# Sliding-window attention and mixture of experts on one core: the value product in 64x64 tiles over two units and two PSUM banks

## Chip, cores and metric

One Trainium2 chip; the kernel runs on 1 core. The metric is the device time of one execution in microseconds (us), smaller is better. Engines are named as in the profile: PE (TensorE), DVE (VectorE), ACT (ScalarE), POOL (GpSimd), SP (the queue that issues most DMAs).

## The reference

```python
# x: (2, 2048, 256) f32; 16 heads of 64; window of 128 keys; 8 experts, top 2
mod = silu(c) @ wmod                     # six rows per batch: shift, scale, gate, twice
h = layernorm(x) * (1 + ca) + sa
q, k, v = split(h @ Wqkv)
scores = q @ k.T * 64 ** -0.5            # key j counts for query i when i-127 <= j <= i
out = softmax(scores) @ v
x = x + ga * (out @ Wout)
h = layernorm(x) * (1 + cb) + sb
x = x + gb * moe(h)                      # gate, top 2 of 8, 640 slots per expert and choice, two products with relu
```

## The kernel before

The 4096 tokens are 8 chunks of 512 (4 tiles of 128). For each chunk the attention runs over 16 units. A unit is a pair of heads j over one half of the chunk: two heads by two query tiles, so four blocks of 128 queries. A block sees 256 keys: the 128 keys before its tile and the 128 of its tile. Exactly half of these 256 are inside the window: key p of the tile before where p > query, key p of the tile itself where p <= query. In the last chunk the units are ordered by half of the chunk first.

There is no scheduler. Each engine has its own instruction stream, written out by hand as a loop over steps i = 4 to 19 in the function `chunk`, and semaphores tie them together. In step i of a chunk before the last:

- **PE** (line 765): `scores` of unit i (fp32, a head's 64 dimensions on one half of the rows, 64 queries on one half of the columns: four 64x64 tiles at once), `weighted_values` of unit i-4, `transposes` of unit i-2 (four 128x128 fp32 transposes of the probabilities into the bank `pt`), then one q or k projection of the next chunk and, in steps 12, 13, 14 and 16, one v projection. Steps 12 and 15 have the router's logits and counts of the chunk before. Behind the last step come four v projections and `project_out`.
- **DVE** (line 1267): in even steps first `attn_low` of a finished pair; then `merge` (i), `invert_sum` (i-1), `row_max` (i), `normalise` (i-1); then what the step has of routing or layer norm (`norm_rows` in step 6, `route_tokens` in 8, `ln_shift` in 9 and 10, `route_softmax` and `route_top` in 13, `route_slots` in 16).
- **ACT** (line 971): `exponentials` (i-1), in odd steps `attn_high`, then `copy_probT` (i-2) from `pt` to SBUF, then the projections' copies out of PSUM. In steps 9 and 11 it also packs 1024 columns for the router and the layer norm.
- **POOL** (line 1438): `split_keys` (i-3), two masked copies of the 512 columns of `probT` into `probT_split` (keys of the tile, keys before it); `route_scale` in 6, `route_shift` in 7, `route_low` in 9, a layer norm part in 12, two scatters a step from 16 on.

The value product (lines 651 to 678) puts v (128 keys, 64 dimensions) in the array as 128x64 tiles, head 0 in the left columns and head 1 in the right, and streams the probabilities: first the middle 256 columns of `probT_split` for both query tiles at once, then the two outer blocks of 128. All 128 keys of every block are multiplied, the masked halves as zeros. It writes the one bank `pv`; a pair of units fills its 512 columns, and only then ACT takes the high half (`attn_high`, 512 columns) and DVE the low half (`attn_low`, 512 columns). The first product of the next pair waits for that:

```python
elif part == 0:
    at_least(pe, attn_lo, PAIRS * c + j)
```

The projections, the logits, the counts and the output products alternate between the two banks `gen0` and `gen1` in the order of the list `chunk_groups` (line 298). `claim` makes PE wait until the group two places back in that list has been copied out of PSUM:

```python
bank, before = group(c, name)
at_least(pe, gen_free[bank], before)
```

The last chunk (c = 7) has leftover projections in steps 4 to 14, and its first output group `("out", 0)` is opened in step 12 and read out by DVE (`add_attention`) in step 14. When its units are done the experts follow, and fill the rest of the time.

## Time and profile before

| | |
|---|---|
| runs | 1147.83, 1148.39, 1149.66 us; median 1148.39 us |
| profiled execution | 1147.24 us, of which the span of the core is 1144.4 us |
| granted TensorE clock, mean | 0.991 |
| busy: PE, DVE, ACT, POOL | 95%, 66%, 58%, 44% of the span |
| attention | about 54 to 691 us of the span: chunks 0 to 5 some 81 to 83 us each, chunk 6 74 us, the last chunk after it |
| experts | from 707 us |

Busy shares are averages over stages with different limits. A matmul's recorded duration includes its way through the array, and neighbours overlap, so the cost of a group on PE is read from the start of one group to the start of the next. In the timelines below the first column is the start in us from the beginning of the span, the second the time from the first start to the last end of the instructions on that row; in brackets the idle time ahead of it on its engine and who ended it.

### The profile page before, as it was taken

Reading aid. Unit: us, or ns where it says so; the run is one execution under the profiler, and the core shown is the slowest. Engines: PE = TensorE matmul, PEld = TensorE weight load, DVE = VectorE, ACT = ScalarE, POOL = GpSimd, SP = SyncE. Lnnn points to the kernel's source line nnn. Section 1 sums busy time; section 2 is a strip of 40 time slices with the busy share of each in tenths; the row PEclk is TensorE's granted clock in tenths of the full one; section 3 lists DMA queues with packets and bytes.
Section 4 is the critical chain, followed back from the end, with each engine's and each line's share of the span. In section 5 each row is a group of like instructions: output and inputs, shape, how many; then the busy total and the mean of one; then the engine's idle time right before and its main releaser. Section 6 shows DMA issues by size and latency. Waiting matters only on the chain.

```text
span 1144.4 us, 25293 instructions
## 1 busy us (share of the span) xinstructions
PE 1084.4 (95%) x9469; PEld 711.8 (62%) x9469; DVE 750.3 (66%) x1663; ACT 660.5 (58%) x1874; POOL 506.2 (44%) x555
## 2 busy tenths in 40 slices
PE   7999999999999999999998885989999999999996
PEld 4455655655655655655656564756776858585765
DVE  5776586586576585674675784756676766666653
ACT  5677476476476476476473853447474563727461
POOL 2234274365275365355445655434344352525342
PEclk9999999999999999999999998999999999999998
DMA  9744111112021021021031024434345353534000
GB/s 335 151 163 138 40 29 48 38 37 52 27 45 48 24 46 45 24 45 39 24 103 48 5 83 121 92 94 81 109 94 153 97 112 111 112 112 78 23 20 9
DMA packets 140114, 87.41 MB, mean 76 GB/s; under 512 B 96708, under 2 KB 130650, under 8 KB 139868
## 3 DMA queue, kind: packets, MB, share of 16 engines
q1 hardware_dynamic: 129244, 64.29, 21.4%
q0 software_dynamic: 10752, 21.54, 6.6%
q8 instruction: 75, 1.23, 0.5%
q14 instruction: 43, 0.35, 0.1%
HBM read 40.02 MB, written 33.79 MB: 64 GB/s over the span
## 4 chain that ended last, share of the span: by engine, by line
PE 75%; issue 7%; DVE 7%; ACT 6%; POOL 4%; DMA 0%; SPq 0%; POOLq 0%; DVEq 0%; ACTq 0%
PE down L1617 18%; PE up L1603 17%; PE gen L600 10%; PE gen L614 7%; PE gen L691 6%; PE score L637 4%; PE pv L668 4%; PE pt L648 4%; ACT prob L909 4%; PE pv L675 3%; DVE prob L1121 2%; POOL h L370 1%; POOL probT_split L1424 1%; PE gen L699 1%; POOL probT_split L1422 1%
## 5 line engine op out<-in xcount | busy, mean ns | idle before, releaser
L1643 ACT ACTIVATE hid<-up,b1T 128x512 f16<-128x512 f32 (+2 forms) x192 | 124.3, 648 | 182.1 <-PE up L1603 180.3
L1603 PE MATMUL up<-xT,w 128*128 128x512 f16 (+2 forms) x1152 | 212.5, 346 | 10.9 <-issue 10.9
L1617 PE MATMUL down<-w,hid 128*128 128x256 f16 x1920 | 213.7, 274 | 3.2 <-DVE hid L1659 3.2
L1422 POOL TENSOR_SCALAR_AFFINE_SELECT probT_split<-probT 128x512 f32<-128x512 f32 x128 | 102.9, 804 | 250.9 <-ACT probT L917 247.4
L1617 PEld LDWEIGHTS down<-w,hid 128*128 128x128 f16 x1920 | 188.6, 98 | 27.6 <-DVE hid L1659 3.7
L600 PE MATMUL gen<-hT,big 128*128 128x512 f16 x768 | 185.0, 380 | 0.6 <-DVE hT L1371 0.6
L909 ACT ACTIVATE prob<-score,negmax 128x128 f32<-128x128 f32 x512 | 180.7, 375 | 0.7 <-DVE negmax L1113 0.7
L1603 PEld LDWEIGHTS up<-xT,w 128*128 128x128 f16 x1152 | 112.9, 98 | 104.9 <-issue 12.8
L1702 POOL DMA_INDIRECT out<-y,tail x80 | 82.4, 1031 | 206.1 <-DVE y L1687 193.2
L1659 DVE TENSOR_TENSOR hid<-hid 128x512 f16<-128x512 f32 (+2 forms) x192 | 115.2, 606 | 72.4 <-ACT hid L1644 72.0
L917 ACT ACTIVATE probT<-pt 128x512 f32<-128x512 f32 x128 | 76.9, 601 | 99.0 <-PE pt L648 98.8
L1109 DVE COPY_PREDICATED score<-above,score 128x512 f32<-128x512 int32 x112 | 77.5, 692 | 77.3 <-PE score L637 77.2
L1644 ACT ACTIVATE hid<-up,b1T 128x512 f32<-128x512 f32 (+2 forms) x192 | 124.8, 650 | 0.0
L600 PEld LDWEIGHTS gen<-hT,big 128*128 128x128 f16 x768 | 73.8, 98 | 67.7 <-issue 1.2
L637 PE MATMUL score<-k,q 64*64 64x192 f32 (+2 forms) x2048 | 111.0, 330 | 2.6 <-issue 2.2
L909 ACT ACTIVATION_READ_ACCUMULATOR prob<-score,negmax 128x1 f32 x512 | 111.0, 217 | 0.0
L1692 POOL DMA_INDIRECT kept<-out,tail x80 | 86.5, 1081 | 47.6 <-issue 30.0
L1121 DVE TENSOR_TENSOR prob<-prob,rinv 128x512 f32<-128x512 f32 x128 | 103.4, 808 | 0.0
L668 PE MATMUL pv<-probT_split,v 128*64 128x256 f32 x512 | 83.5, 403 | 19.0 <-DVE attn L1134 7.0
L637 PEld LDWEIGHTS score<-k,q 64*64 64x64 f32 x2048 | 64.5, 132 | 53.9 <-issue 51.6
L614 PE MATMUL gen<-big,hT 128*128 128x512 f16 x384 | 89.1, 379 | 2.3 <-DVE logit L1160 1.2
L1424 POOL TENSOR_SCALAR_AFFINE_SELECT probT_split<-probT 128x512 f32<-128x512 f32 x128 | 86.3, 674 | 0.0
(159 smaller groups left out, 1442.4 us busy)
## 6 DMA issues: line engine op xcount, KB each, us to landing
big<-in_L_ffn_W SPq DMA_DIRECT2D x14, 1024.0 KB, 6.9
slot_inputs<-empty_row SPq DMA_DIRECT2D x80, 129.5 KB, 2.3
out<-x SPq DMA_DIRECT2D x7, 512.0 KB, 3.3
x<-in_L_attn_x SPq DMA_DIRECT2D x1, 3072.0 KB, 22.8
k<-k SPq DMA_DIRECT2D x48, 64.0 KB, 1.9
kept<-out,tail POOLq DMA_INDIRECT x80, 3.1
out<-y,tail POOLq DMA_INDIRECT x80, 2.4
x<-in_L_attn_x SPq DMA_DIRECT2D x2, 512.0 KB, 6.9
```

The source lines that it names most:

```text
L600: mm = pe.matmul(dst[:], wqkv[:, kd, a, col:col + P], hT[:, cn % 2, kd, b, :], start=(n == 0), stop=(n == 5))
L614: mm = pe.matmul(dst[:], hT[:, cn % 2, kd, a, s * P:(s + 1) * P], wqkv[:, kd, b, 2 * INNER + half * 512:2 * INNER + (half + 1) * 512], sta ...
L637: mm = pe.matmul(dst[lo:lo + HALF, 2 * hd + i, first:lo + P + HALF], q[r:r + DH, j, b * P + lo:b * P + lo + HALF], k[r:r + DH, j, b * P + ...
L668: mm = pe.matmul(pv[r:r + DH, 2 * part * P:(2 * part + 2) * P], v[:, 2 * part + 1, h * DH:(h + 1) * DH], probT_split[:, par, 2 * hd:2 * hd ...
L909: mm = act.activation(prob[:, h % 2, b, :], score[h % 2][:, b, P:], ACT.Exp, bias=negmax[:, h % 2, b:b + 1], accum_out=rowsum[:, h % 2, b: ...
L1121: dve.tensor_tensor(prob[:, h % 2], prob[:, h % 2], rinv[:, h % 2, :].unsqueeze(2).to_broadcast([P, TILES, P]), ALU.mult)\
L1422: pool.affine_select(out=probT_split[:, h % 2, :, 1], in_=probT[:, h % 2], pattern=[[0, TILES], [1, P]], compare_op=ALU.is_ge, fill=zero, ...
L1603: mm = pe.matmul(bank, w1[:, par, kd, a, ft * P:(ft + 1) * P], part_rows(e, n, xT[:, par, b * KD + kd, :]), start=(i == 0), stop=(i == 5))
L1617: mm = pe.matmul(down[n][:, s, :], hid[:, ft, a, t * P:(t + 1) * P], w2[:, par, ft, b, :], start=(i == 0), stop=(i == 3 * FT - 1))
L1643: act.activation(part_rows(e, n, hid[:, ft, 0, :]), bank, ACT.Relu, scale=1 / W_SCALE, bias=bias).then_inc(hid_hi, 1)
L1644: act.activation(part_bank(e, n, hid32[:, k_ % 4, :]), bank, ACT.Relu, scale=1 / W_SCALE, bias=bias).then_inc(up_out, 1)
L1659: dve.tensor_tensor(part_rows(e, n, hid[:, ft, 1, :]), part_bank(e, n, hid32[:, k_ % 4, :]), part_rows(e, n, hid[:, ft, 0, :]), ALU.subtra ...
```

## The change

It does six things.

1. The value product is cut into 64 keys by 64 dimensions. `high_keys` are keys 64 to 127, `low_keys` keys 0 to 63. Where a 64x64 quarter of a block is wholly masked it is left out: high keys of the tile itself see only queries 64 to 127, low keys of the tile before only queries 0 to 63. So a block's four products have 128, 64, 128 and 64 columns.
2. In one step PE runs the high keys of unit i-4 mixed, one by one, with the low keys of unit i-5 (`half_values`), so that all four quarters of the array have work, and the two halves of the rows write to different banks. In the first step of a chunk only the new unit is there; in the last step the mixed product comes ahead of the scores and the last unit's low keys alone behind them.
3. `pv` becomes two banks, one unit each (256 columns). ACT's and DVE's part is done for every unit (`attn_high_part`, `attn_low_part`), one step later than before, DVE's at the head of every step. A product waits for the low half of the unit two back.
4. For the second `pv` bank, `pt` goes: the transposes are groups of the `gen` banks now, ahead of the step's other groups.
5. `probT` goes: ACT copies the transposes straight into slot 1 of `probT_split`, a ring of three units, and POOL masks from there, the second time in place.
6. The v projections of steps 12, 13, 14, 16 move to 13, 14, 16, 17; `keep_v` from step 12 to 13. The last chunk keeps the old product of 128x64 tiles, with the new banks. (The key copies that the change's short name speaks of are transfers of the sync queue before and after.)

```diff
-                        if c == LAST:
-                            at_least(pe, attn_lo, PAIRS * c + u)
-                        elif part == 0:
-                            at_least(pe, attn_lo, PAIRS * c + j)
+                        at_least(pe, attn_lo, n_unit - 1)
...
+                    def high_keys(c, u, hd, i, cur):
...
+                        first = HALF * cur
+                        return pe.matmul(pv[n_unit % 2][r:r + DH, i * P + first:(i + 1) * P], v[HALF:, b + cur, h * DH:(h + 1) * DH],
+                                         probT_split[HALF:, n_unit % RING, 2 * hd + i, cur, first:], start=(i == 0 and cur == 0),
+                                         stop=False, skip_group_check=True)
...
+                    def low_keys(c, u, hd, i, cur):
...
+                        last = P if cur else HALF
+                        return pe.matmul(pv[n_unit % 2][r:r + DH, i * P:i * P + last], v[0:HALF, b + cur, h * DH:(h + 1) * DH],
+                                         probT_split[0:HALF, n_unit % RING, 2 * hd + i, cur, 0:last], start=False,
+                                         stop=(cur == 0), skip_group_check=True)
...
+                        for i in range(2):
+                            for n in range(2):
+                                for hd in range(2):
+                                    if new is not None:
+                                        high = high_keys(c, new, hd, i, n)
+                                    if old is not None:
+                                        low = low_keys(c, old, 1 - hd, i, 1 - n)
...
+                            if not last and i == STEPS[-1]:
+                                half_values(c, i - HI_AT, i - LO_AT)
                             if i < H or not last:
                                 scores(c, i)
-                            weighted_values(c, i - 4)
+                            if last:
+                                weighted_values(c, i - HI_AT)
+                            elif i < STEPS[-1]:
+                                half_values(c, i - HI_AT, i - LO_AT if i >= LO_AT else None)
+                            else:
+                                half_values(c, None, H - 1)
                             if i - 2 < H or not last:
-                                transposes(c, i - 2)
+                                transposes(H * c + i - 2, c, ("pt", i))
...
                         for i in STEPS:
-                            if i >= 6 and i % 2 == 0 and not last:
-                                attn_low(c, (i - 6) // 2)
+                            if i > LO_AT and not last:
+                                attn_low_part(c, i - LO_AT - 1)
```

**How the order moves.** Three places, as the instruction streams have them; line numbers are each kernel's own.

DVE, chunk 2, step 6 and the head of step 7, before (L237 is `norm_rows`; L1109, L1117, L1113 and L1121 are merge, invert_sum, row_max and normalise; L1134 is `attn_low`):

```order
L1134 TENSOR_TENSOR attn<-pv,attn 128x512 [waits attn_hi]
L1109 COPY_PREDICATED score<-above,score 128x4x128 [waits scores_done]
L1117 RECIPROCAL rinv<-rowsum 128x4 [waits exp_done]
L1113 TENSOR_REDUCE negmax<-score 128x4 [waits merged]
L1121 TENSOR_TENSOR prob<-prob,rinv 128x512 [waits rinv_ready]
L237 TENSOR_SCALAR h<-x,meanvar,rstd 128x256 [waits r_rstd]
L237 TENSOR_SCALAR h<-x,meanvar,rstd 128x256 x3
L1109 COPY_PREDICATED score<-above,score 128x4x128 [waits scores_done]
```

The same place after (L1291 is `attn_low_part`):

```order
L1291 TENSOR_TENSOR attn<-pv,attn 128x256 [waits attn_hi]
L1158 COPY_PREDICATED score<-above,score 128x4x128 [waits scores_done]
L1166 RECIPROCAL rinv<-rowsum 128x4 [waits exp_done]
L1162 TENSOR_REDUCE negmax<-score 128x4 [waits merged]
L1170 TENSOR_TENSOR prob<-prob,rinv 128x512 [waits rinv_ready]
L236 TENSOR_SCALAR h<-x,meanvar,rstd 128x256 [waits r_rstd]
L236 TENSOR_SCALAR h<-x,meanvar,rstd 128x256 x3
L1291 TENSOR_TENSOR attn<-pv,attn 128x256 [waits attn_hi]
L1158 COPY_PREDICATED score<-above,score 128x4x128 [waits scores_done]
```

Behind the routing work of every step there now stands a low half that PE waits for, also in the odd steps.

PE, chunk 2, step 12, before (L648 transposes, L740 logits, L600 a q projection, L614 a v projection):

```order
L648 MATMUL pt<-identf,prob 128x128 [waits probT_ready,norm_ready]
L648 MATMUL pt<-identf,prob 128x128 x3
L740 MATMUL gen<-gate,h2T 128x8 [waits gen_free0,turned]
L740 MATMUL gen<-gate,h2T 128x8 x23
L600 MATMUL gen<-hT,big 128x512 [waits gen_free1]
L600 MATMUL gen<-hT,big 128x512 x5
L614 MATMUL gen<-big,hT 128x512 [waits gen_free0]
L614 MATMUL gen<-big,hT 128x512 x5
L637 MATMUL score<-k,q 64x192 [waits exp_done]
```

The same place after, where the last rows show the mixed product behind the scores:

```order
L654 MATMUL gen<-identf,prob 128x128 [waits gen_free0,norm_ready]
L654 MATMUL gen<-identf,prob 128x128 x3
L783 MATMUL gen<-gate,h2T 128x8 [waits gen_free1,turned]
L783 MATMUL gen<-gate,h2T 128x8 x23
L607 MATMUL gen<-hT,big 128x512 [waits gen_free0]
L607 MATMUL gen<-hT,big 128x512 x5
L644 MATMUL score<-k,q 64x192 [waits exp_done]
L644 MATMUL score<-k,q 64x192 x7
L674 MATMUL pv<-probT_split,v 64x128 [waits cur_ready,attn_lo,prev_ready,high_done]
L683 MATMUL pv<-probT_split,v 64x128
L674 MATMUL pv<-probT_split,v 64x128
```

The projection waits for the bank that the same step's transposes filled a moment before. Step 15 has the same with the counts in place of the logits.

PE, last chunk, steps 13 and 14, after (L742 is the output product into `("out", 0)`, which lies in `gen0`):

```order
L742 MATMUL gen<-wout,attn 128x256 [waits attn_lo]
L742 MATMUL gen<-wout,attn 128x256 x26
L644 MATMUL score<-k,q 64x192 [waits exp_done]
L644 MATMUL score<-k,q 64x192 x7
L712 MATMUL pv<-probT_split,v 64x256 [waits attn_lo,cur_ready,prev_ready]
L712 MATMUL pv<-probT_split,v 64x256
L718 MATMUL pv<-probT_split,v 64x128 x4
L654 MATMUL gen<-identf,prob 128x128 [waits gen_free0,norm_ready]
```

The transposes of step 14, which had a bank of their own, now wait until DVE has read the output group out.

## Rows read from the trace of the kernel before

**Rows 1.** Windows: busy us of each engine (count), clock, DMA share, GB/s
```profile
140.00:220.00 80.00, 78.32 (x756) 48.28 (x758) 52.87 (x130) 49.98 (x177) 41.11 (x47) 1.00 0.13 34
```
**Rows 2.** Waits of PE in chunk 2, 218.7 to 302.05
```profile
PE pv L668 <- POOL probT_split L1424: 0.8, 2, 0.6
PE pv L668 <- DVE attn L1134: 0.7, 2, 0.5
PE gen L614 <- DVE logit L1160: 0.2, 1, 0.2
```
**Rows 3.** Timeline of PE, chunk 3, step 4 and the next step's start
```profile
302.06 0.88 PE L637 MATMUL score<-k,q 64*64 64x192 f32 x16
302.87 0.65 PE L668 MATMUL pv<-probT_split,v 128*64 128x256 f32 x4
303.35 0.61 PE L675 MATMUL pv<-probT_split,v 128*64 128x128 f32 x8
303.89 0.66 PE L648 MATMUL pt<-identf,prob 128*128 128x128 f32 x4
304.38 1.46 PE L600 MATMUL gen<-hT,big 128*128 128x512 f16 x6
305.77 0.55 PE L637 MATMUL score<-k,q 64*64 64x192 f32 x7
```
**Rows 4.** Timeline of PE, chunk 4, step 4: narrower score tiles at a batch's start
```profile
385.16 0.77 PE L637 MATMUL score<-k,q 64*64 64x64 f32 x16
385.86 0.65 PE L668 MATMUL pv<-probT_split,v 128*64 128x256 f32 x4
```
**Rows 5.** Groups by line and form: busy us, mean ns of one
```profile
L931 ACT ACTIVATE attn<-pv 128x256 f16<-128x256 f32 x16 | 6.3, 391 | 21.0 <-PE pv L675 21.0
...
L1246 DVE TENSOR_TENSOR attn<-pv,attn 128x256 f16<-128x256 f32 x16 | 6.7, 418 | 2.3 <-ACT attn L931 2.3
```
**Rows 6.** Timeline of ACT, chunk 3, step 5, whose scores start at 309.48
```profile
311.36 0.22 ACT L909 ACTIVATION_READ_ACCUMULATOR prob<-score,negmax 128x1 f32 x1
312.01 0.60 ACT L917 ACTIVATE probT<-pt 128x512 f32<-128x512 f32 x1 [0.43 <-PE pt L648]
```
**Rows 7.** Timeline of DVE, the same step
```profile
311.61 0.18 DVE L1117 RECIPROCAL rinv<-rowsum 128x4 f32<-128x4 f32 x1 [0.48 <-ACT prob L909]
...
312.29 0.68 DVE L1121 TENSOR_TENSOR prob<-prob,rinv 128x512 f32<-128x512 f32 x1
```
**Rows 8.** Timeline of PE, chunk 2: scores of step 6, values of steps 8, 9
```profile
226.15 0.88 PE L637 MATMUL score<-k,q 64*64 64x192 f32 x16
...
235.07 0.65 PE L668 MATMUL pv<-probT_split,v 128*64 128x256 f32 x4 [0.61 <-POOL probT_split L1424]
...
239.02 0.65 PE L668 MATMUL pv<-probT_split,v 128*64 128x256 f32 x4 [0.17 <-POOL probT_split L1424]
```
**Rows 9.** Timeline of DVE, chunk 2: norm_rows of step 6, normalise and ln_shift of 10
```profile
229.55 1.38 DVE L237 TENSOR_SCALAR h<-x,meanvar,rstd 128x256 f32<-128x256 f32 x4
...
244.77 1.12 DVE L1121 TENSOR_TENSOR prob<-prob,rinv 128x512 f32<-128x512 f32 x1
245.81 1.62 DVE L1080 SCALAR_TENSOR_TENSOR xn<-xn,rstd,kept 128x256 f32<-128x256 f32 x2
```
**Rows 10.** Timeline of POOL, chunk 2: route_scale, and the select after route_shift
```profile
231.02 2.37 POOL L370 TENSOR_TENSOR h<-h,modrow 128x1024 f32<-128x1024 f32 x1 [4.02 <-DVE h L237]
...
238.34 0.63 POOL L1424 TENSOR_SCALAR_AFFINE_SELECT probT_split<-probT 128x512 f32<-128x512 f32 x1
```
**Rows 11.** Timeline of DVE, chunk 2, step 13: route_top, then attn_low of step 14
```profile
259.00 0.18 DVE L1175 TENSOR_REDUCE lsum<-logit 128x4 f32<-128x32 f32 x1
...
261.16 0.69 DVE L1134 TENSOR_TENSOR attn<-pv,attn 128x512 f16<-128x512 f32 x1
```
**Rows 12.** Timeline of PE, last chunk, step 14
```profile
675.97 0.66 PE L648 MATMUL pt<-identf,prob 128*128 128x128 f32 x4
```
**Rows 13.** Timeline of DVE, last chunk, step 14: add_attention reads the output group
```profile
677.36 0.68 DVE L1142 SCALAR_TENSOR_TENSOR gated<-gen,modrow 128x512 f32<-128x512 f32 x1
```

More of the change, by code:

```diff
@@ L325, in group, with turned_in @@
                 return bank, opened[c][bank] + before
+            def turned_in(n_unit):
+                c, i = divmod(n_unit - 2, H)
+                return group(-1, ("pt", n_unit)) if n_unit < 2 else group(c, ("pt", i + LAG))
             def starts_batch(c, b):
@@ L846, in attention_tensor @@
                     pe.wait_ge(mod_row, 1)
-                    transposes(0, 0)
+                    transposes(0, -1, ("pt", 0))
                     scores(0, 2)
@@ L906, in exponentials @@
                         act.wait_ge(maxed, u + 1)
-                        at_least(act, pt_done, u - 1)
+                        if u >= 2:
+                            bank, before = turned_in(u - 2)
+                            act.wait_ge(gen_full[bank], before + 1)
                         for b in range(TILES):
@@ L976, in chunk @@
                             if last:
-                                attn_high_part(c, i - 4)
-                            if i % 2 == 1 and not last:
-                                attn_high(c, (i - 5) // 2)
+                                attn_high_part(c, i - HI_AT)
+                            if i >= LO_AT and not last:
+                                attn_high_part(c, i - LO_AT)
                             if last and i - 2 < H:
@@ L1277, in chunk @@
                                 keep_first_keys((i - LAG) // 2)
-                            if i == 12 and not last:
+                            if i == 13 and not last:
                                 keep_v(c, 0)
@@ L1309, in chunk @@
                         if not last:
-                            attn_low(c, PAIRS - 1)
+                            for u in range(H - 2, H):
+                                attn_low_part(c, u)
                             keep_v(c, 1)
```

131 lines of the change are left out of this document (72 added, 59 removed).

## Prediction

> **What bounds the kernel now.** First the windows: in a stretch of the middle chunks PE is busy 78.3 of 80 us, DVE 52.9, ACT 50.0 and POOL 41.1 [rows 1]. PE is the bound there. Then the waits of PE: in the 83 us of chunk 2 only 1.7 us are waits, for POOL's selects, DVE's low half and the logits' bank [rows 2]. So what is taken off PE arrives in full, as long as it isn't waited away again. The change touches the attention alone (chunks 0 to 6 in full, the last in its banks); the experts behind it stay as they are. Third the timeline of one step, from start to start [rows 3]: scores 0.81, value product 0.48 + 0.54 = 1.02, transposes 0.49, one projection 1.39, in all 3.71 us.
>
> **The value product.** The price of a column in fp32: at a batch's start two of the four passes of a score group are 128 columns wide in place of 192, and the group takes 0.70 in place of 0.81 us [rows 3, 4]. So 128 columns cost 0.11 us, 0.83 ns each, and a pass costs what its widest tile costs. (Every fp32 product is two passes; the records count them.) A score group is 4 passes of 192, 768 columns, 0.64 us; measured 0.81. The value product is now 2 passes of 256 and 4 of 128, 1024 columns, 0.85 us; measured 1.02. So each group that changes the tile's shape pays some 0.17 us, a first load and a drain.
> The mixed product has, for each quarter of the array, passes of 128, 128, 64, 64 and the same again: 768 columns, 0.64 us. It has the scores' shape and follows them directly, so the two pay 0.17 once: 0.64 + 0.64 + 0.17 = 1.45 for 1.83. That is 0.38 us a step, and a step of 3.33. What isn't shown is a pass of 64 columns. Its bounds: 0.05 us as its columns say, or 0.11 as a pass of 128, if the next load doesn't fit under it; then the product takes 8 x 0.107 = 0.85. I take the first, because the transposes, 128 columns loaded for 128 streamed, run four in 0.49 us [rows 3], hardly more than their 0.43 of columns: a load fits under as many columns as it loads.
> Sixteen steps in seven chunks give 112 x 0.38 = 42.6 us. The skew costs one product more in each chunk (first high, last low alone), 7 x 0.64 = 4.5. **38 us of work go from PE, if nothing else becomes late.**
> The rule that speaks against this is in the Trainium skill, TensorE: Matmul & The Clock Gate, Part 3, "Packing small matmuls": a weight load overlaps a running matmul only where it goes to another row group. In the mixed product all quarters are busy, so by that rule each of the eight passes would show its load.
>
> **What ACT, DVE and POOL get.** DVE's low half goes from one of 512 columns per pair, 0.69 [rows 11], to two of 256 at 0.42 [rows 5], under 0.1 us more per step; ACT's high half likewise, at 0.39. Both engines have that much room under PE's 3.33 [rows 1]. POOL's two selects stay.
> But their order now matters. In a quiet step ACT's exponentials end 2.1 us after the scores' start (309.48), DVE inverts at 2.13, normalises from 2.81 to 3.49 [rows 6, 7], and the low half of 0.42 ends at 3.9. The product of the next step is due at 3.33 + 0.70 = 4.03. There is 0.1 us to spare, where before a low half was due only every second step. So **all that DVE does in a step behind the normalisation is now waited for in full, in odd steps too**. Once PE has waited, DVE is ahead by as much in the next step.
>
> **A middle chunk, wait by wait** (chunk 2; times from the scores of step 6, 226.15 [rows 8]):
> - Step 7: `norm_rows` starts at 3.40 and takes 1.38 [rows 9], then the low half, done at 5.15; the product is due at 4.03. Wait 1.1.
> - Steps 8 and 9: `norm_rows` starts POOL's chain: scale, selects, shift, selects, which end at 8.9 and 12.8 [rows 10]. PE follows at 8.92 and 12.87 [rows 8]. DVE and POOL don't depend on PE's pace here, so these two instants stay. PE, faster and held in step 7, would be there at 8.5 and 12.25: waits 0.4 and 0.6. The whole gain of steps 6 to 9 is gone.
> - Step 11: `ln_shift` of step 10 takes 1.62, two instructions beside POOL's selects; at `norm_rows`'s pace (1.38 for four of the same width) two would take 0.7 [rows 9]. So the wait is between 0.5 and 1.6; I take 1.4, because the selects follow ACT's copy, whose place in the step hardly moves.
> - Step 12: logits come between the transposes and the projection, which needs the transposes' bank. ACT is through with the exponentials at 2.1, the high half at 2.45, the copy of 0.60 at 3.05 [rows 5, 6]; the projection is due at 2.5. Wait 0.55.
> - Step 14: `route_top`, 2.16 us from its first instruction to the low half [rows 11], behind a normalisation that ends 3.5 after the scores and with `route_softmax` and `keep_v` ahead of the step's merge; the product, behind one more projection, is due at 5.3 and gets its low half at about 6.05: 0.75.
> - Step 15: the counts do as the logits, projection due at 2.3: 0.8.
> - Step 19: the product comes ahead of the scores, so due 0.7 earlier: 0.5.
> Sum 6.1. Before there were 1.7 [rows 2], from start to start 2.0 (the wait of 0.61 in step 8 makes 8.92 out of 2 x 3.71 + 0.81 = 8.23, 0.07 more, and so the others). So 4.1 us of new waits. The chunk's work shrinks by 16 x 0.38 - 0.64 = 5.4. **Net 1.3 us.**
>
> **The sum.**
> - Chunk 0 (no routing; `ln_shift` 0.15 more, step 19 0.5): 5.4 - 0.65 = 4.8.
> - Chunks 1 to 5: 5 x 1.3 = 6.3.
> - Chunk 6: steps 4 to 13 as above without `ln_shift`, 3.8 - 2.0 = 1.8. From 14 on it has no projections and is bound by DVE, ACT and POOL's scatters; half a step's gain, 0.7. Together 2.5.
> - Last chunk: the transposes of step 14 start at 675.97 [rows 12], now only after DVE has read the output group, 677.36 + 0.68 = 678.04 [rows 13]. Scores, exponentials and the router's second round hang on it: -2.1.
> 11.5 us less: the profiled execution, 1147.24, becomes 1135.8. The median of the runs is 1.1 above it, so **1137 us**.
>
> **Rivals.**
> A, the new waits are half as long: one wait gives DVE and ACT time that the next needs less, and `ln_shift` misses POOL's selects. For it: each wait is a small difference of two long sums. Against: steps 8 and 9 are fixed by what was measured. Half of 4.1 x 5 is 10 us: 1126, chance 0.17.
> B, a pass of 64 columns costs one of 128: product 0.85, step 3.54. Chunk 0 loses 17 x 0.21 = 3.6 and gets back 0.4 of waits; a middle chunk loses 10 x 0.21 outside steps 6 to 11 and gets back 0.8; chunk 6 some 1.2. In all 11 us, so no change: 1148, chance 0.13.
> C, on the other side: DVE's tail paces PE in every step. POOL's selects begin at 3.1, inside the normalisation (2.81 to 3.49) [rows 6, 7], and where they meet it took 1.12 in place of 0.68 [rows 7, 9]. Then the low half ends at 4.35, and each step without a v projection is 0.3 longer; it decides from 0.1 us of delay on. Twelve steps in chunk 0, seven in each of 1 to 5, ten in chunk 6: 57 x 0.3 = 17 us, 1154. Against: in the quiet step shown the two meet and 0.68 was measured. Chance 0.13.
> D, each load is shown: the value product's first group has 2 x 256 columns, 0.43, and takes 0.48, so a shown load is 0.05 us. Eight make the product 1.04 and the step 3.73, which is no gain; the extra product (7 x 1.04), steps 12 and 15 (some 3) and the last chunk's 2.1 remain: 1160, chance 0.04. By the Trainium skill's rule above this is what would come. The passes of 128 in the value product, four in 0.54 with the drain [rows 3], speak against it, since they use the same rows and show no load.
> E, the halves of the rows don't run together: product 1.28, step 3.97, 0.26 worse than now. 112 x 0.26 less a part hidden in waits, some 27 us: 1175, chance 0.03. The scores use the same four quarters and pay 768 columns, not 1536.
>
> **How the numbers follow.** My forecast, 1137, has chance 0.50; its own range, from the bounds of `ln_shift` and the waits, is 1130 to 1144. The range for 8 in 10 takes in A, B and C's middle: 1125 to 1154. Faster by over 0.2% (2.3 us, about what can be told from no change here): the forecast and A, 0.67. Within 0.2%: B and a sliver, 0.14. Slower: C, D, E less that sliver, 0.19.
>
> **What would show it.** In the profile after: from scores to mixed product 0.70, from there to the transposes 0.74, a quiet step 3.33. PE's waits for DVE's low half at 5 us a chunk, with those behind `norm_rows`, `ln_shift` and `route_top` the longest; waits for ACT's copy in steps 12 and 15; the product of step 9 still 12.9 us after the scores of step 6; the last chunk's transposes waiting 2 us for `add_attention`. Chunk 0 should gain most. A mixed product of 0.95 or a quiet step of 3.6 would prove me wrong; so would middle chunks that gain 4 us.

## The result, and the profile after

| | before | after |
|---|---|---|
| median of the runs | 1149.03 us (4 runs, 1147.83 to 1151.04) | 1160.65 us (4 runs, 1159.95 to 1163.68) |
| ratio | | 1.0104, 95% interval 1.008 to 1.0128 |
| profiled execution, span | 1147.24, 1144.4 us | 1159.95, 1158.1 us |

The change makes the kernel 12 us slower; the forecast was 1137. Two executions far outside the rest, 3855.89 us of old_product and 1415.90 us of all3_old_product, are left out of the medians below. From the page of the changed kernel, its span, busy times and two rows of the slices (the second is the granted clock in tenths):

```profile
span 1158.1 us, 29868 instructions
...
PE 1067.1 (92%) x11709; PEld 730.9 (63%) x11709; DVE 754.9 (65%) x1719; ACT 667.4 (58%) x1930; POOL 509.8 (44%) x555
...
PE   7999988988989988988998884989999999999996
...
PEclk9999999999999999999999997999999999999998
```

PE is busy 17 us less (1084.4 before) and yet ends 13.7 us later: work went, and about 30 us of waiting came. The timeline of PE in a quiet step, chunk 3 step 4, which answers to [rows 3]:

```profile
304.00 0.88 PE L644 MATMUL score<-k,q 64*64 64x192 f32 x16
304.71 0.28 PE L674 MATMUL pv<-probT_split,v 64*64 64x128 f32 x2
...
305.47 0.66 PE L654 MATMUL gen<-identf,prob 128*128 128x128 f32 x4
305.97 1.46 PE L607 MATMUL gen<-hT,big 128*128 128x512 f16 x6
307.36 0.88 PE L644 MATMUL score<-k,q 64*64 64x192 f32 x16
```

Scores to mixed product 0.71, to the transposes 0.76, the step 3.36 us: the cut product costs what the prediction said. The records of single passes say the same: one of 64 columns starts 0.05 us before the next, one of 128 columns 0.11. PE's waits in all, and then in chunk 2 alone (us in total, times, longest), where [rows 2] had 1.7 us:

```profile
PE pv L674 <- DVE attn L1291: 26.1, 33, 2.1
...
PE gen L621 <- ACT probT_split L970: 8.1, 8, 1.4
...
PE pv L674 <- POOL probT_split L1468: 4.2, 12, 0.6
PE gen L607 <- ACT probT_split L970: 3.8, 10, 0.4
```

```profile
PE pv L674 <- DVE attn L1291: 3.3, 5, 1.7
PE gen L621 <- ACT probT_split L970: 2.2, 2, 1.4
PE gen L607 <- ACT probT_split L970: 0.8, 2, 0.4
PE pv L674 <- POOL probT_split L1468: 0.6, 2, 0.4
```

From the starts of the score groups, chunk by chunk (us from one chunk's first scores to the next's; the last row runs to the end of the span):

| | before | after | forecast of the difference | measured |
|---|---|---|---|---|
| up to chunk 0 | 54.4 | 55.0 | 0 | +0.6 |
| chunk 0 | 80.95 | 78.12 | -4.8 | -2.8 |
| chunks 1 to 5 | 416.4 | 427.1 | -6.3 | +10.7 |
| chunk 6 | 73.77 | 74.92 | -2.5 | +1.2 |
| last chunk and experts | 518.8 | 523.0 | +2.1 | +4.2 |

Most of the miss, 17 of 25 us, lies in chunks 1 to 5. Three places in chunk 2 were not in the forecast. First, step 9. DVE's rows, then POOL's:

```profile
240.21 2.68 DVE L1129 SCALAR_TENSOR_TENSOR xn<-xn,rstd,kept 128x256 f32<-128x256 f32 x2
242.81 0.41 DVE L1291 TENSOR_TENSOR attn<-pv,attn 128x256 f16<-128x256 f32 x1
```

```profile
240.45 2.16 POOL L386 TENSOR_TENSOR packed<-h,packed 128x1024 f16<-128x1024 f32 x1 [1.47 <-ACT packed L991]
```

The second of the two layer norm shifts is held until POOL's subtraction ends (0.48 and 2.28 us; the pair of the next step takes 0.88). The low half stands behind them, and step 10 takes 1.95 us more than a quiet one. Before, the same pair met the same subtraction and lost nothing:

```profile
241.37 0.88 DVE L1080 SCALAR_TENSOR_TENSOR xn<-xn,rstd,kept 128x256 f32<-128x256 f32 x2
```

```profile
241.78 2.39 POOL L379 TENSOR_TENSOR packed<-h,packed 128x1024 f16<-128x1024 f32 x1 [1.64 <-ACT packed L943]
```

There the second shift starts at 241.76, 0.02 us ahead of the subtraction, and takes 0.48; after the change it starts at 240.60, 0.15 us behind it. In chunks 1, 2, 3 and 5 the changed kernel has it behind. In chunk 4 the second shift is 0.10 us ahead and isn't held; the pair of step 10 then meets the selects, as in the rows of before (1.62, [rows 9]), and step 11 takes 5.40. With a margin of 0.02 us, the kernel before was lucky.

Second, step 17. ACT's rows of chunk 2; "remote" is a wait whose releaser the profile can't place:

```profile
274.98 0.22 ACT L961 ACTIVATION_READ_ACCUMULATOR prob<-score,negmax 128x1 f32 x1
276.55 0.38 ACT L979 ACTIVATE attn<-pv 128x256 f16<-128x256 f32 x1 [1.35 <-remote]
277.29 0.60 ACT L970 ACTIVATE probT_split<-gen 128x512 f32<-128x512 f32 x1 [0.35 <-remote]
277.79 0.59 ACT L944 ACTIVATE k<-gen 128x512 f32<-128x512 f32 x1
```

The product that ACT waits for was issued by 274.42. The trace also has the instant at which a semaphore is raised. Between the start of a matmul and its event lie, in chunk 2 (us):

```
                                  before, step 17      after, step 17
last of the value product         276.89  + 0.30       274.41  + 2.12
last of the transposes            277.47  + 0.29       274.96  + 2.31
last of the k projection          278.66  + 0.39       276.15  + 1.19
```

PE's rows go on meanwhile, up to its v projection, which has to wait for ACT's copy; it is the news that comes late. This happens in steps 17, 18 and 19 of chunks 1 to 6 (of chunk 1 in 18 and 19), beside POOL's scatters: 65 events come over 0.43 us behind their matmul in the changed kernel, none in those chunks before. ACT's own events are on time (0.01 us behind their instruction). I call the 65 **late events** below. They lengthen step 17 of chunk 2 by 1.6 us and the end of the chunk by 0.9. Chunk 0 of the same trace, which has no scatters, shows steps 17 to 19 without them: 28.34 us, where chunks 1 to 5 take 30.2 to 30.9, 11.4 us more in all. (The kernel before takes 26.80 in chunk 0 and 26.7 to 26.8 in chunks 1 to 5.)

Third, the last chunk. PE's timeline at step 14, where [rows 12] stood, and the windows around it (busy time of each engine, then the granted clock):

```profile
687.45 0.65 PE L654 MATMUL gen<-identf,prob 128*128 128x128 f32 x4 [2.14 <-DVE gated L1187]
687.92 2.74 PE L621 MATMUL gen<-big,hT 128*128 128x512 f16 x6
690.59 1.23 PE L644 MATMUL score<-k,q 64*64 64x192 f32 x16
```

```profile
684.00:687.90 3.90, 1.76 (x24) 1.18 (x17) 3.51 (x7) 0.38 (x1) 0.00 (x0) 1.00 0.08 28
687.90:691.30 3.40, 3.40 (x19) 1.30 (x20) 0.13 (x1) 1.20 (x3) 2.20 (x3) 0.50 0.23 77
```

The wait is the forecast's 2.1 us to the digit. But behind it PE gets a granted clock of 0.5, 1.2 GHz, for 3.4 us, and the projection takes 2.74 instead of 1.46. Leaving out the last 10 us of the span, PE ran at the lower level for 13.6 us before and 23.9 us after; one of the new stretches is at 612.8, behind a 2.1 us wait in chunk 6.

### The profile page after: what moved, and what is told of

It is laid out like the page before. It is cut to its first block, busy times and chain, and to the rows that moved or that the text cites. A ratio compares the mean times of both kernels' runs of the same rounds, so it can differ in the third digit from the quotient of the medians.

```text
span 1158.1 us, 29868 instructions
## 1 busy us (share of the span) xinstructions
PE 1067.1 (92%) x11709; PEld 730.9 (63%) x11709; DVE 754.9 (65%) x1719; ACT 667.4 (58%) x1930; POOL 509.8 (44%) x555
## 4 chain that ended last, share of the span: by engine, by line
PE 67%; DVE 10%; ACT 9%; issue 7%; POOL 4%; another core or an unknown queue 1%; DMA 1%; SPq 1%; DVEq 0%; ACTq 0%
PE up L1647 16%; PE down L1661 16%; PE gen L607 9%; PE gen L734 6%; PE gen L621 6%; ACT prob L961 5%; PE gen L654 4%; PE score L644 3%; PE pv L683 2%; PE pv L674 2%; DVE prob L1170 2%; DVE negmax L1162 1%; POOL h L377 1%; DVE xn L1129 1%; ACT probT_split L970 1%
## 5 line engine op out<-in xcount | busy, mean ns | idle before, releaser
L1647 PE MATMUL up<-xT,w 128*128 128x512 f16 (+2 forms) x1152 | 212.9, 346 | 11.5 <-issue 11.5
L1466 POOL TENSOR_SCALAR_AFFINE_SELECT probT_split<-probT_split 128x512 f32<-128x512 f32 x128 | 107.1, 837 | 253.2 <-ACT probT_split L970 249.4
L1647 PEld LDWEIGHTS up<-xT,w 128*128 128x128 f16 x1152 | 113.1, 98 | 105.6 <-issue 13.6
L970 ACT ACTIVATE probT_split<-gen 128x512 f32<-128x512 f32 x128 | 78.4, 612 | 86.6 <-PE gen L654 85.4
L674 PE MATMUL pv<-probT_split,v 64*64 64x64 f32 (+1 forms) x1792 | 97.9, 247 | 30.4 <-DVE attn L1291 26.1
L674 PEld LDWEIGHTS pv<-probT_split,v 64*64 64x64 f32 x1792 | 91.6, 134 | 48.8 <-issue 48.1
L683 PE MATMUL pv<-probT_split,v 64*64 64x128 f32 (+1 forms) x1792 | 98.6, 248 | 0.5 <-remote 0.5
L1170 DVE TENSOR_TENSOR prob<-prob,rinv 128x512 f32<-128x512 f32 x128 | 98.2, 767 | 0.0
```

The lines of the kernel that those rows point to most:

```text
L674: return pe.matmul(pv[n_unit % 2][r:r + DH, i * P + first:(i + 1) * P], v[HALF:, b + cur, h * DH:(h + 1) * DH], probT_split[HALF:, n_unit ...
L683: return pe.matmul(pv[n_unit % 2][r:r + DH, i * P:i * P + last], v[0:HALF, b + cur, h * DH:(h + 1) * DH], probT_split[0:HALF, n_unit % RIN ...
L1170: dve.tensor_tensor(prob[:, h % 2], prob[:, h % 2], rinv[:, h % 2, :].unsqueeze(2).to_broadcast([P, TILES, P]), ALU.mult)\
L1647: mm = pe.matmul(bank, w1[:, par, kd, a, ft * P:(ft + 1) * P], part_rows(e, n, xT[:, par, b * KD + kd, :]), start=(i == 0), stop=(i == 5))
```

## The experiments

Ratios are to the kernel before, run on the same chip, with 95% intervals. Differences in us between two experiments are of their medians; where these ran on different chips, the ratios can give some 2 to 3 us more or less.

**1. old_product** (and, for its rows, **old_product_look**, since the only profile of the first is that of the 3855.89 us). All chunks call the product of before:

```
-   half_values(c, i - HI_AT, i - LO_AT if i >= LO_AT else None)
+   weighted_values(c, i - HI_AT)
```

> The changed kernel with the product of before (128 keys by 64 dimensions, one unit a step, no extra product in a chunk's last step) in all chunks; its banks, its copies and its drains per unit stay. Theory 1 (the cut product is as cheap as its price says, 0.38 us a step, and the loss comes from waits that the new banks and drains bring): the price comes back, 5.4 us a chunk, less what the longer steps absorb, about 0.38 us in each of the nine steps of a middle chunk where PE waits now, 3.4: some 87.5 us a middle chunk and 1172 to 1185 us in all, well above both kernels. Theory 2 (the cut product costs what the old one did, and the banks cost nothing): 1149 to 1153 us. Theory 3 (another engine paces the steps, whatever PE does): 1160 us, as the changed kernel.

1169.97 us, ratio 1.0178 (1.0155 to 1.0201). Just below theory 1's interval. So banks, drains and the order, with the late events that come with them, cost some 20 us here, and the cut product takes back 9.

> The kernel of old_product once more, for its rows (128x64 tiles, one unit a step, the new banks and drains). In the changed kernel the events that PE's matmuls post come late three times a chunk, in steps 17, 18 and 19 of chunks 1 to 6, up to 2.1 us behind the matmul that posts them, beside POOL's scatters, and ACT stands still for them; in the kernel before none comes over 0.4 us late. Theory S (the many short matmuls of the cut product beside the scatters hold the events up): none is late here, step 17 takes as long as step 16. Rival (the banks or the drains per unit do it): three a chunk as before, 1.5 to 2.1 us each. The time is 1169 to 1173 us by the other runs.

1175.15 us in its one run. Neither: two late events of the product a chunk are left in chunks 1 to 5, of 1.2 us mostly, where there were two or three of 1.5 to 2.7. So the cut product is not needed for them. `ln_shift` met POOL here too (3.10 us for the pair) and PE waited 2.3 us in step 10.

**2. low_early.** DVE's low half goes behind the normalise:

```
-   if i > LO_AT and not last: attn_low_part(c, i - LO_AT - 1)
    softmax_step(c, i, last)
-   if last: attn_low_part(c, i - 4)
+   if i >= LO_AT: attn_low_part(c, i - (HI_AT if last else LO_AT))
```

> The changed kernel with DVE's low half of unit i-5 right behind its normalise in step i, ahead of the routing and the layer norm, instead of at the head of step i+1 behind them. Theory 1 (PE waits for that low half because it stands behind DVE's routing and layer norm work, 26.1 us in 33 waits): most of these waits go, a middle chunk falls from 85.6 to 82 or 83 us, and the time to 1137 to 1146 us. Theory 3 (DVE or POOL paces these steps anyway, and PE would wait for the next thing): waits of the same size for the masked copies or the scores' merge stand in their place, 1156 to 1161 us.

1154.19 us, 1.0032 (1.0018 to 1.0047): 6.5 us, a third of what was expected. Its waits of PE:

```profile
PE pv L674 <- DVE attn L1291: 18.4, 21, 2.2
...
PE pv L674 <- POOL probT_split L1467: 9.8, 13, 1.5
...
PE gen L621 <- ACT probT_split L970: 8.1, 8, 1.4
```

A third of the low half's waits went (that of step 10 moved to step 11), and 5.6 us came back as waits for POOL's selects, in step 8. The 66 late events stayed. Both theories have a part.

**3. add_early.** `"add": 14` becomes `"add": 13` in the last chunk.

> The changed kernel with DVE's addition of the first projected tiles at the end of the last chunk's step 13 instead of step 14, so that the general bank is free before PE's transposes of step 14. Theory 1 (the 2.1 us wait of these transposes, and the 3.4 us at half clock right behind it, are one cause): step 14 falls from 7.2 to between 3.6 and 4.0 us, the granted clock stays full there, and the time falls by 3 to 4 us, to 1157 us. Rival (the wait alone, the clock falls from the phase of the work and not from this wait): 2 us, 1158.5. Second rival (PE waits for the rest of the chunk anyway): 1160 to 1161 us.

1159.87 us, 1.0085 (1.0068 to 1.0102), 0.8 us. Step 14 took 3.71 us and its clock stayed full, as expected, and still the time hardly moved. Two rows of its windows say why:

```profile
695.30:698.70 3.40, 1.19 (x14) 0.70 (x10) 3.37 (x8) 1.24 (x4) 3.10 (x5) 1.00 0.80 279
698.70:702.10 3.40, 2.92 (x22) 2.10 (x22) 1.75 (x4) 0.93 (x2) 3.06 (x5) 0.50 0.07 23
```

PE, earlier by 3.5 us, waits for DVE and then for POOL's selects in the next thin place (0.79 and 1.91 us; busy 1.19 of 3.4 us), and the clock falls there. My expectation took the fall for part of this one wait; it moves to where the work is thin.

**4. groups_late.** In a middle chunk, logits and counts behind their step's projection, on PE and in the list that hands out the banks:

```
+   if ahead:                       # steps 12 and 15, chunks 1 to 6
+       for name in projections_at(c, i): project(c, name)
    if not first and i == at["logits"]: route_logits(c)
```

> The changed kernel with the router's logits and counts of a middle chunk (steps 12 and 15) behind the projection of their step instead of ahead of it, so that the transposes and that projection lie in different banks. Theory 1 (in these two steps PE waits for ACT's copy of the transposes because three groups share two banks, 3.8 us in all): 0.4 to 0.5 us a chunk less in each of the two steps, 1156 to 1158 us. Rival (the wait moves to DVE, which gets logits and counts 1.3 us later): 1160 to 1163 us.

1156.67 us, 1.0062 (1.0042 to 1.0081): 4.0 us, as theory 1 said. Step 12 went from 4.55 to 4.07 and step 15 from 4.32 to 3.70; steps 13 and 14 gave back 0.65, the rival's part. Late events fell from 65 to 50, though nothing near the scatters was touched but the instant at which PE gets there.

**5. scatters_end.** POOL's scatters behind the chunk's last step:

```
-   if not first and not last and at["send"] <= i < at["send"] + TILES:
-       scatter(c, [i - at["send"]])
...
    if not first and not last:
+       for s in range(TILES): scatter(c, [s])
```

> The changed kernel with POOL's eight scatters of a middle chunk behind its last step, beside the v projections and the output product, instead of two a step in steps 16 to 19 beside the cut product. Theory S (cut product beside scatters holds up PE's events): steps 17 to 19 lose their late events, 1.6 us in step 17 and 0.9 us in the rest of the chunk, 2.5 us in each of the chunks 1 to 5 and some 2 in chunk 6, 1144 to 1149 us. Rival (the events come late wherever scatters run): the same 2 us gaps move into the chunk's end, where ACT's copies of v wait for them, 1158 to 1163 us. Second rival (the events come late in these steps whatever POOL does): no change, 1160 us.

1188.79 us, 1.0325 (1.0272 to 1.0379), worse than any theory. Steps 17 and 18 lost their excess (4.66 and 4.66 us), so theory S had that right. So the late events go where the scatters go. But beside eight scatters in a row they came up to 6.8 us late, the end of a chunk grew from 20 to between 24 and 27 us, and PE stood before the v projections:

```profile
PE gen L621 <- issue: 25.8, 8, 5.6
```

Part of the growth is the clock: behind these waits the granted clock was 0.50 for 3.4 to 6.8 us in each of chunks 1 to 6 (in chunk 2 from 294.1 to 300.9).

**6. shift_apart.** `LN_AT = (8, 10)` in place of `(9, 10)`.

> The changed kernel with the first half of DVE's layer norm shift in step 8 instead of step 9. Theory C (in step 9 DVE's two shifts, 0.88 us elsewhere, are held 2.68 us by POOL's subtraction that starts 0.24 us after them, and PE's 1.9 us wait in step 10 for the low half behind them is that): the pair takes 0.9 us, the wait in step 10 falls from 1.9 to under 0.3 us, 1.5 us or more in each of chunks 0 to 5, so 1150 to 1153 us. Rival (the step is paced by DVE's other work): the wait stands in step 9 or 10 with over 1 us, 1158 to 1161 us.

1168.34 us, 1.0163 (1.0135 to 1.019); the profiled one, the quickest, 1165.77. The rival, and worse: the pair in step 8 meets the selects (1.70), the one in step 10 too (1.62), and steps 9 and 11 take 1.9 and 1.5 us more than a quiet one. POOL works through most of steps 6 to 10, so a pair moved by a step meets something else.

**7. all5.** All five moves.

> The changed kernel with five moves together: low halves right behind the normalise, the addition of the last chunk a step earlier, logits and counts behind the projection, scatters behind the last step, first shift in step 8. If the waits are what costs (theories 1, S and C), a middle chunk comes to 79.5 to 81 us, against 85.6 in the changed kernel and 83.3 in the one before, and the time to 1126 to 1136 us, below both kernels. If another engine paces these steps (theory 3), waits come back elsewhere and it stays at 1142 to 1150 us.

1166.53 us, 1.0138 (1.011 to 1.0167). Steps 4 to 18 of chunk 2 took 60.9 us against 65.8 in the changed kernel, as the theories said; the end of the chunk 25.4 against 20.0, by scatters_end's late events and half clock. The bad move hid four good ones.

**8. no_scatters, before_no_scatters, before_scatters_end.** The first two leave out POOL's scatters of chunks 1 to 6 and lower the waits on their count, so their output isn't that of the reference; the third is scatters_end's edit on the kernel before. These ran together, with all3, on another chip than everything above.

> The changed kernel with POOL's scatters of chunks 1 to 6 left out (48 of 56; the rows of the first six chunks reach no expert, so the output is that of a kernel without them; the experts' work keeps its size). Theory S (scatters hold up PE's events in this kernel): no event of a middle chunk comes over 0.4 us late, steps 17, 18 and the chunk's end fall by 1.6 and 0.9 us, and chunks 1 to 6 by some 2.5 us each, to 1144 to 1147 us. Rival (they come late without scatters too): 1158 to 1161 us.

1149.21 us, 0.9977 (0.9953 to 1.0002). Late events of chunks 1 to 6: one, in step 11. Step 17 4.65, the chunk's end 19.03 us, chunks 1 to 5 416.9 us, 10.2 less; steps 17 to 19 of these chunks are 11.5 us shorter, as chunk 0 of the changed kernel said (11.4), and a stretch at a granted clock of 0.50 (413.3 to 416.7) made steps 4 to 16 of chunk 4 some 1.3 longer. The time is 11.4 us less by the medians (14.6 by the ratios), 2 to 5 us short of what was expected. The changed kernel itself wasn't run beside it, so this run alone doesn't show that leaving out the scatters took the late events away; see the end of experiment 11.

> The kernel before with the same scatters left out. No event of PE comes late in it with the scatters, so if those cost it nothing: 1147 to 1150 us, chunks of 83.3 us. If they cost it something that its rows do not show: 1140 to 1145 us.

1150.46 us, 0.9991 (0.9962 to 1.0019).

> The kernel before with its eight scatters a chunk behind the last step, as in scatters_end. If the scatters hold up PE's events whatever kernel they run in, and the kernel before only has them where they meet none: PE's events come 4 us late at the end of chunks 1 to 6 here too, and it loses what scatters_end lost, some 28 us, 1170 to 1180 us. If it is the changed kernel's banks, drains or products that make them late: 1147 to 1152 us.

1148.49 us, 0.9989 (0.9965 to 1.0012), no late event. Neither differs from the kernel before, whose chunks 1 to 5 take 416.4 us in all three traces; only chunk 6 is 1.0 and 1.4 us shorter. The kernel before had no late event with its scatters where the changed one had 65, so scatters alone don't make events late.

**9. all3.** low_early, add_early and groups_late together.

> The changed kernel with the three moves that helped, low_early, groups_late and add_early. If their gains add (6.5, 4.0 and 0.8 us): 1149 to 1150 us, level with the kernel before. If one takes what another gave (DVE's tail is one queue for the low halves and the logits): 1152 to 1154 us.

**1133.52 us, 0.9852 (0.9805 to 0.99)**, 27 us less than the changed kernel where the three alone gave 11.2, and better than either expectation. Middle chunks take 81.0 us, the chunk's end 19.03, step 17 4.66. Seven late events are left, the longest 0.55 us. Of the 22.1 us that chunks 1 to 5 gained, 10.7 lie in steps 4 to 16, where the moves act, and 11.4 in steps 17 to 19, where the late events were. So most of what came beyond the sum is late events that are gone; whether the three moves took them away isn't shown (end of experiment 11).

**10. all3_old_product.** Experiment 1's edit on all3.

> all3 with the product of before (128x64 tiles) in all chunks. In a kernel whose events are not late this shows what the cut product is worth. Theory 1 (0.38 us a step, 5.4 us a chunk net of the extra product in the last step, by the price of the prediction; four waiting steps a chunk absorb up to 0.35 us each): middle chunks of some 85 us against 81.0, and 1155 to 1162 us, above the kernel before. Theory 2 (the cut product is worth no more than the 10 us between old_product and the changed kernel): 1141 to 1146 us.

1149.73 us, 1.0015 (1.0 to 1.0031), no late event: between the two. The cut product is worth 1.6% here, 16 us by the medians and 19 by the ratios, of the 38 forecast. And the new banks and drains, in this order and without late events, cost next to nothing. Chunk 2 step by step, against all3: 15 steps of 3.36 for 3.71 and an end of 19.03 for 19.40 give 5.6; the extra product takes back 1.3; the waits, 4.1 us with it and 2.2 without, take back 1.9. 2.4 is left, and 83.39 - 80.97 was measured.

**11. scatters_first, all3_scatters_first.** The scatters of steps 17 to 19 ahead of `split_keys`.

> The changed kernel with POOL's scatters of steps 17 to 19 ahead of the two masked copies of their step instead of behind them, so that they start about 1.3 us earlier against PE's product. If the late events depend on where a scatter meets PE's step: their number changes, from 65 in chunks 1 to 6 to under 20, and the time goes to 1146 to 1152 us, if the masked copies, 2.6 us later, are still in time for the product. If they come with this kernel's scatters wherever those stand: 50 or more late events, 1158 to 1166 us.

1153.82 us, 1.0043 (1.0028 to 1.0059); late events from 65 to 7. Chunks 1 to 5 are at 417.2 us, as without scatters; chunk 6 lost 3.4, with two waits of PE for POOL's selects in step 18 (1.7 and 1.4 us) and a granted clock of 0.50 for 13.7 us, against 3.4 in the changed kernel.

> all3 with the scatters ahead of the masked copies, as in scatters_first. all3 has 7 late events, the longest 0.6 us. If where a scatter meets PE's step decides: over 20 late events come back here and the time goes up by 5 us or more, to 1138 to 1150 us. If the order of DVE's low halves or of the groups decides (what all3 changed): none comes back, 1131 to 1136 us.

1139.12 us, 0.9922 (0.9899 to 0.9945), one late event. Neither: they don't come back, and the 5.6 us are selects that come later (step 18 5.22 for 4.66 us, and more in chunk 6).

**Does the place of a scatter decide?** The traces say no. In chunk 2 of groups_late and of all3 the scatters of steps 17 and 18 start at the same points of PE's step, to 0.02 us (2.0 and 3.3, 1.1 and 2.4 us behind the scores). Step 18 of groups_late has four late events, of 1.0 to 2.7 us; step 18 of all3 has two, just over the limit (0.44 and 0.49). What does divide the runs is when they were made. Every changed kernel of experiments 1 to 7 and the changed kernel itself had 30 or more late events; every kernel run after them had at most seven, whatever its edit, and the changed kernel was never run again beside these. The record of semaphore events differs in the same way: 9005 to 9189 of them in the traces with late events, 10475 to 11467 in all others, and the missing ones begin with the first scatters. It isn't the chip alone, since all4_tail ran on the one that scatters_end had used. So each edit from no_scatters on is compared with a kernel of an earlier set, and that an edit removed the late events is possible, not shown. One more run of the changed kernel beside them would tell. Whether the profiler has a part in them isn't shown either.

**12. all4.** all3 and shift_apart.

> all3 with the first half of the layer norm shift in step 8 (shift_apart). In all5 PE's wait in step 11 was 0.1 us with it, in all3 it is 1.4 us, and the steps 4 to 18 of a middle chunk take 60.9 against 61.9 us. If no event comes late: 1.0 us less in each of chunks 0 to 5, 1126 to 1129 us. If the shift of 1 us brings the scatters back to where PE's events come late: 2 us more a chunk, 1138 to 1148 us.

1128.42 us, 0.9832 (0.9806 to 0.9857), in the expected interval. The move that cost 8 us on the changed kernel (7 by the ratios) gives 5 here (2 by the ratios, which are on two chips); in the traces chunks 1 to 5 take 400.0 for 405.0, with step 11 at 3.50 for 4.84.

**13. all4_tail.** In a chunk's last step the scores come first, then the mixed product, the transposes, and the last unit's low keys.

> all4 with the last step's products in another order: scores, mixed product of units 15 and 14, transposes, then the low keys of unit 15 alone, instead of the mixed product ahead of the scores. In the changed kernel and in all4 the step ahead of it takes 1.3 us more than a quiet one where the extra product is 0.64 us: the rest is PE standing between its projection and the mixed product, for the low half of unit 13, which DVE has only 0.6 us later. If that is so, the new order gives 0.6 us in each of chunks 0 to 6, 4 us, 1123 to 1126 us. If PE then waits as long for ACT's copy or for the low half at the output product: 1127 to 1130 us.

**1123.93 us, 0.9788 (0.977 to 0.9806)**, as expected, the fastest: 24 us below the kernel before. Steps 18 and 19 together took 23.33 in place of 23.69 us; so of the 0.66 us a half was that wait. From its page and its waits of PE:

```profile
span 1123.2 us, 29868 instructions
...
PE 1060.5 (94%) x11709; PEld 732.7 (65%) x11709; DVE 759.3 (68%) x1719; ACT 663.7 (59%) x1930; POOL 516.2 (46%) x555
```

```profile
PE pv L675 <- POOL probT_split L1470: 11.2, 14, 1.5
...
PE pv L675 <- DVE attn L1294: 6.9, 10, 2.1
```

The same instructions as in the changed kernel, to the number, in another order; what PE waits for most is now POOL's selects.

## Why the prediction was wrong

Right were the prices. A pass of 64 columns costs its columns; 0.70 from scores to product (measured 0.71), 3.33 for a step (3.36). Rivals B, D and E fall with that: the product is not 0.85, 1.04 or 1.28. By the rule in the Trainium skill, TensorE: Matmul & The Clock Gate, Part 3, "Packing small matmuls", each load would show. This trace doesn't agree: from the first row of the mixed product to the transposes there are 0.76 us, and the prediction's own estimate with eight shown loads was 1.04. In the sum, 5 x 1.3 was entered as 6.3; exactly it is 6.5, which changes nothing.

The waits of a middle chunk, step by step (chunk 2; excess over a quiet step, over 4.66 us where there is a v projection, and in steps 12 and 15 over the same steps of all3, 3.94 and 3.70 us):

| step | forecast | measured | what it is |
|---|---|---|---|
| 6 | 0 | 0.77 | low half; DVE busy 6.15 of the 6.18 us before it |
| 7 | 1.1 | 0.48 | low half behind `norm_rows` |
| 8, 9 | 0.4, 0.6 | 0.49, 0.60 | POOL's chain; product of step 9 at 13.1 us (forecast 12.9) |
| 10, 11 | 0, 1.4 | 1.95, 0 | `ln_shift` |
| 12, 15 | 0.55, 0.8 | 0.61, 0.62 | ACT's copy |
| 14 | 0.75 | 0.82 | `route_top` |
| 17 | 0 | 1.58 | late events |
| 18, 19 | 0.5 | 0.70 | mixed product ahead of the scores |
| end of chunk | 0 | 0.93 | late events |
| sum | 6.1 | 9.55 | |

The 3.45 us between the sums and 16 x 0.03 for the quiet step are, to 0.3 us, what lies between a gain of 1.3 and a loss of 2.4.

1. **The step that failed most is the one that isn't there.** "Net 1.3 us" had no term for events that reach ACT late, 2.5 us in this chunk. Nothing in the rows of before showed any, and none of the rivals named it. In the changed kernel's own trace they are worth 11.4 of the 17 us that chunks 1 to 5 missed the forecast by (steps 17 to 19 against those of chunk 0). Without them these chunks would take 415.7 us against 416.4 before: level, and still not the 6.3 us of gain. The rest of the miss is the points that follow.
2. **"Step 11: `ln_shift` of step 10 ... between 0.5 and 1.6; I take 1.4."** The mechanism was right, the neighbour wrong. I bounded it by the row beside POOL's selects. In the new kernel the other pair, step 9's, lost the race with `route_low` that it had won by 0.02 us before, and was held to the end of it: 2.68 us, wait 1.95, above my bound. In chunk 4, where it won, the forecast's wait came in step 11, with 2.0 for 1.4.
3. **Step 6** had no wait in the forecast. DVE comes out of the chunk's end late, with the output's addition and then `norm_stats`, and works without a gap up to the low half (one window of the changed kernel; DVE is the third busy time):

```profile
219.80:225.98 6.18, 6.07 (x86) 3.77 (x84) 6.15 (x18) 4.24 (x16) 3.47 (x5) 1.00 0.29 95
```

Before, that low half ended at 226.53, 0.4 us ahead of PE's product (scores at 226.15 [rows 8], and 0.81). Now it ends at 226.25 and the product is due at 225.68. The sum started each step from a quiet one, and this stretch was never quiet.
4. **"Last chunk: -2.1."** The wait was there, 2.14 us. The term lacked the half clock behind it: step 14 took 7.18 us for 3.71, of which 2.14 are the wait and the other 1.3 the clock. add_early took both away and the fall came later in the chunk, so it isn't tied to this wait.
5. **Chunk 0, "-4.8"**, came to -2.8. The wait of 1.5 us in step 10 isn't new, 1.3 of it stood there before; what the sum lacked is 0.3 in step 11, 0.85 in step 13, where DVE does `ln_shift` and `keep_v`, and 16 times 0.03 for the quiet step. I had allowed 0.15 and 0.5. low_early gave 1.2 us back by taking the wait out of step 10.
6. **Chunk 6, "-2.5"**, came to +1.2: late events, a 2.1 us wait for the low half and the clock at 612.8.

Rival C said that DVE's tail paces PE in every step, for 1154. Its sign was right, its mechanism only in steps 6 to 11: in the quiet steps 4 and 5 nothing waits. The forecast's claim that a faster PE wouldn't change what DVE and POOL do held in steps 8 and 9, for which it was made; in step 10 the order of the two changed. What decides it for the reader: by the quiet step some 35 us of work went (112 x 0.35 less the extra products), and a gain of 17 us appeared when the order of the rest was made for it and no event came late, of 24 with two moves more.

Open is what makes events late. Shown: they come beside the scatters and move with them (scatters_end, run beside shift_apart, which kept them in steps 17 to 19); the scatters aren't enough (none in the kernel before); the cut product isn't needed (old_product_look); where in PE's step a scatter falls doesn't decide (groups_late and all3). Not shown: that leaving out or moving the scatters, or shorter steps 6 to 15, take them away, since all the runs without them are of later sets in which the changed kernel is missing. Which part of the new banks, drains or waits brings them wasn't tried apart.

## What to carry to other kernels

Work taken off the bounding engine must be costed together with the order of the engines that feed it: list for each step what stands ahead of the piece it waits for, and put that piece first. Judge single moves by the step table and not by the total alone, because a move can be worth -8 us before the others are made and +5 us after, and one bad move can hide four good ones. A wait on PE of some 2 us may cost more than itself through the clock, so look at the granted clock behind each new wait. And when an experiment removes an effect, run the kernel that had the effect once more beside it: here that run is missing, and half of the best result hangs on it.

## What the runs showed of the hardware

- Beside indirect DMAs issued by POOL, semaphore events of PE came up to 2.7 us behind the start of their matmul (0.18 to 0.39 us otherwise), and up to 6.8 us with eight such DMAs in a row, in the changed kernel and seven variants of it; in the kernel before and in all kernels run later, most with the same DMAs, hardly any did.
- Of two DVE operations on 128x256 fp32 in a row, 0.48 us each, one that started behind a POOL operation on 128x1024 took 2.28 us, to POOL's end, and one that started 0.02 us ahead of it took 0.48. Those that started behind one of POOL's selects took 0.85 to 0.93 us.
- After a stretch in which PE was busy 1.76 of 3.9 us, the granted clock was 0.50 for 3.4 us, and six projection matmuls took 2.74 instead of 1.46 us. With that wait gone it fell later in the chunk, behind 1.19 busy of 3.4.
- 64x64 tiles on all four quarters of the array, with 64 or 128 columns, ran at the price of their columns: a mixed product of 768 columns fits in 0.76 us with its drain.
